# A two-layer graph convolution after a graph attention layer, 6250 nodes and 100000 edges: more buffers for the one-hot matrices and more accumulator banks

## The reference

```python
# GAT: weights a per edge and head (softmax over the edges of one node)
msg = feat_v[src] * a[:, :, None]
rst = jax.ops.segment_sum(msg, dst, num_segments=N)
# GCN layer, twice (x = relu(_gcn_layer(x, W, b, ...)))
h = x @ W
deg = jax.ops.segment_sum(ones, dst, num_segments=n_nodes) + SELF_LOOP_W
dinv = jnp.where(deg > 0, jax.lax.rsqrt(deg), 0.0)
msgs = h[src] * (dinv[src] * dinv[dst])[:, None]
agg = jax.ops.segment_sum(msgs, dst, num_segments=n_nodes)
return agg + h * (SELF_LOOP_W * dinv * dinv)[:, None] + b
```

## Time and profile before

| what | us |
|---|---|
| median of 3 runs | 5063.07 |
| span of the profiled execution | 5032.2 |
| GAT aggregation, about 899 to 2254 | 1355 |
| first GCN aggregation, about 2471 to 3645 | 1174 |
| second GCN aggregation, about 3850 to 5021 | 1171 |

### The profile page before, as it was taken

How to read it: one execution, slowest core, us unless ns; L and a number is a source line. 1 busy time by engine, 2 the same in 40 slices (tenths; PEclk the granted TensorE clock), 3 DMA queues, 4 the chain that set the end, 5 groups by cost and what they waited for, 6 DMA issues and landing times.

```text
span 5032.2 us, 77636 instructions
## 1 busy us (share of the span) xinstructions
PE 3834.1 (76%) x18550; PEld 2250.0 (45%) x18551; DVE 2339.5 (46%) x4398; ACT 2192.4 (44%) x5340; POOL 2436.2 (48%) x2548
## 2 busy tenths in 40 slices
PE   4679998667667667779777777777897777777777
PEld 3369983455555555554323333333343333333333
DVE  5358887556566566668422222222353222222226
ACT  3236542334344444445444444444543444444444
POOL 3510000555555555543466666666503666666666
PEclk8889999888888888889888888899998888888989
DMA  7522325555555555555566665666514666666668
GB/s 247 169 60 59 84 53 182 153 158 156 154 157 152 143 146 146 151 146 196 185 178 181 174 177 170 170 177 174 158 75 144 182 178 179 175 170 172 177 174 305
DMA packets 317266, 803.60 MB, mean 160 GB/s; under 512 B 67665, under 2 KB 97251, under 8 KB 316241
## 3 DMA queue, kind: packets, MB, share of 16 engines
q0 software_dynamic: 193760, 629.95, 43.7%
q1 hardware_dynamic: 94981, 120.30, 7.6%
q10 hardware_dynamic: 28428, 52.40, 3.1%
HBM read 718.21 MB, written 85.04 MB: 160 GB/s over the span
## 4 chain that ended last, share of the span: by engine, by line
PE 56%; another core or an unknown queue 17%; issue 12%; ACT 6%; DVE 3%; ACTq 2%; DMA 2%; DVEq 1%; SPq 1%; POOL 1%; POOLq 0%
PE mm L1661 12%; PE tr L1661 11%; PE mm L1491 7%; PE mm L1638 4%; PE sm L1638 4%; PE mm L1583 4%; PE tr L1583 4%; ACT eler_hots L1392 2%; PE sm L1528 2%; ACT eler_hots L1383 2%; PE tr L1638 2%; PE hist_ps L1638 2%; PE tr L1486 1%; DVE big L857 1%
## 5 line engine op out<-in xcount | busy, mean ns | idle before, releaser
L1250 POOL DMA_INDIRECT edge<-h_tab,src_group x1564 | 1491.3, 954 | 1079.9 <-issue 431.7
L1392 ACT ACTIVATE eler_hots<-eler_hots,ones 128x256 f32<-128x256 f32 x1320 | 663.8, 503 | 1177.8 <-remote 622.4
L1661 PE MATMUL mm<-edge,eler_hots 128*128 x1760 | 923.3, 669 | 308.5 <-ACT eler_hots L1392 152.5
L1661 PE MATMUL tr<-edge,eler_hots 128*128 x1760 | 916.5, 664 | 277.8 <-DVE big L857 109.4
L1250 POOL DMA_INDIRECT rows_wmat<-v_tab,src_group x782 | 739.0, 945 | 636.7 <-DVE edge L831 375.8
L1383 ACT ACTIVATE eler_hots<-iota,ndrel 128x128 f32<-128x128 f32 x2640 | 916.0, 393 | 173.8 <-issue 9.1
L1661 PEld LDWEIGHTS mm<-edge,eler_hots 128*128 128x128 f32 x1760 | 367.4, 214 | 835.9 <-issue 830.7
L1661 PEld LDWEIGHTS tr<-edge,eler_hots 128*128 128x128 f32 x1760 | 364.9, 212 | 799.7 <-issue 799.7
L857 DVE TENSOR_TENSOR big<-big,mm 128x512 f32 x440 | 302.8, 688 | 894.3 <-remote 347.1
L857 DVE TENSOR_TENSOR big<-big,tr 128x512 f32 x440 | 302.7, 688 | 827.8 <-remote 371.0
L1638 PE MATMUL mm<-edge,eler_hots 128*128 128x260 f32 x1176 | 423.3, 446 | 308.7 <-ACT eler_hots L1392 206.5
(11 more groups left out here) (234 smaller groups left out, 3873.8 us busy)
## 6 DMA issues: line engine op xcount, KB each, us to landing
h_tab<-rows_wmat SPq DMA_DIRECT2D x98, 256.0 KB, 2.0
edge<-h_tab,src_group POOLq DMA_INDIRECT x1564
rows_wmat<-low_tab SPq DMA_DIRECT2D x191, 128.0 KB
ht_tab<-rows_wmat SPq DMA_DIRECT2D x49, 256.0 KB
big<-ht_tab ACTq DMA_DIRECT2D x49, 256.0 KB
v_tab<-rows_wmat ACTq DMA_DIRECT2D x49, 256.0 KB
x_tab<-big SPq DMA_DIRECT2D x49, 256.0 KB, 2.1
rows_wmat<-v_tab,src_group POOLq DMA_INDIRECT x782
```

What stands on the lines that cost most here:

```text
L1250: pool.indirect_dma_start(ring[:, 2 * u + c, :], None, tab, bass.IndirectOffsetOnAxis(ap=src_group[:, n:n + 1], axis=0)).then_inc(a["rows_ ...
L1392: act.activation(onehot[:, s.j % 2, :, :], dist[:, :, :], ACT.Relu, bias=ones[:, 0:1], scale=-1.0).then_inc(a["onehot_set"], 1)
L1661: last = pe.matmul(sum_ps[bank][:, :], onehot[:, s.j % 2, n, :], edge[:, ds(slot[0][s.j] + n * D, D)], start=(n == 0), stop=(n == 1))
```

## The change

`hots` is a new tile of 8 KB per partition with eight one-hot buffers; `dist` gets two buffers, in the room that the one-hots leave in `eler_hots`. In the GCN the Relu of step n waits for `step_sum` n - 7 (step n - 8 has been summed) and the Abs of step n for the Relu of step n - 2. The GCN accumulators go round eight banks, so PE waits for `acc_added` of the step eight before. In the GAT the accumulators stay three pairs; there the one-hot is tied to the three `msgs` buffers, whose last 8 columns ACT writes at the same point, and the Relu of step n waits for step n - 3 to be summed. Loops grow where the buffer number has to be fixed in the code: ACT's in the GCN from 4 to 8 steps, PE's in the GAT from 12 to 24.

```diff
+SUMS = 8
+HOTS = 8
...
+        hots = sb("hots", [P, HOTS * 2 * P])
...
-        onehot = eler_hots[:, 0:4 * P].rearrange("p (b c n) -> p b c n", b=2, c=2)
-        dist = eler_hots[:, 4 * P:6 * P].rearrange("p (c n) -> p c n", c=2)
+        onehot = hots[:, :].rearrange("p (b c n) -> p b c n", b=HOTS, c=2)
+        dist = eler_hots[:, 0:4 * P].rearrange("p (b c n) -> p b c n", b=2, c=2)
...
         sum_ps, half_ps = mm + tr, sm + [hist_ps, misc]
+        agg_ps = sum_ps + half_ps
...
-                        w, bank = s.k - LAG, (s.j - LAG) % BANKS
+                        w, bank = s.k - LAG, (s.j - LAG) % SUMS
...
-                        dve.tensor_tensor(big[:, ds(o, D)], big[:, ds(o, D)], sum_ps[bank][:, :], ALU.add).then_inc(a["acc_added"], 1)
+                        dve.tensor_tensor(big[:, ds(o, D)], big[:, ds(o, D)], agg_ps[bank][:, :], ALU.add).then_inc(a["acc_added"], 1)
...
-                    if s.past(1):
-                        act.wait_ge(a["onehot_set"], n)
+                    reuse = MSGS if a["weighted"] else HOTS
+                    if s.past(2):
+                        act.wait_ge(a["onehot_set"], n - 1)
                     for c in range(2):
-                        act.activation(dist[:, c, :], iota[:, :], ACT.Abs,
+                        act.activation(dist[:, s.j % 2, c, :], iota[:, :], ACT.Abs,
...
-                    if s.past(2):
-                        act.wait_ge(a["step_sum"], n - 1)
+                    if s.past(reuse):
+                        act.wait_ge(a["step_sum"], n - reuse + 1)
...
-                    pipelined(act, SP, 4, 0, step, tail=(SP - SETTLED) * bool(settled))
+                    pipelined(act, SP, HOTS, 0, step, tail=(SP - SETTLED) * bool(settled))
...
-                            last = pe.matmul(bank_ps[:, 0:hi - lo], onehot[:, s.j % 2, n, :], msgs[:, s.j % MSGS, n, lo:hi],
+                            last = pe.matmul(bank_ps[:, 0:hi - lo], onehot[:, s.j % HOTS, n, :], msgs[:, s.j % MSGS, n, lo:hi],
...
-                pipelined(pe, SP, 4 * PAIRS, 0, step)
+                pipelined(pe, SP, HOTS * PAIRS, 0, step)
...
-                    if s.past(BANKS):
-                        pe.wait_ge(a["acc_added"], w - BANKS + 1)
+                    if s.past(SUMS):
+                        pe.wait_ge(a["acc_added"], w - SUMS + 1)
                     for n in range(2):
-                        last = pe.matmul(sum_ps[bank][:, :], onehot[:, s.j % 2, n, :], edge[:, ds(slot[0][s.j] + n * D, D)],
+                        last = pe.matmul(agg_ps[bank][:, :], onehot[:, s.j % HOTS, n, :], edge[:, ds(slot[0][s.j] + n * D, D)],
```

More of the change, by code:

```diff
@@ L1390, in step @@
                                        ACT.Copy)
-                    act.activation(onehot[:, s.j % 2, :, :], dist[:, :, :], ACT.Relu,
+                    act.activation(onehot[:, s.j % HOTS, :, :], dist[:, s.j % 2, :, :], ACT.Relu,
                                    bias=ones[:, 0:1], scale=-1.0).then_inc(a["onehot_set"], 1)
@@ L1646, in step @@
                 def step(s):
-                    w, bank = s.k, s.j % BANKS
+                    w, bank = s.k, s.j % SUMS
                     if s.j == 0:
```

## The result

The kernel after takes **5020.13 us** (median of 5 runs, 5009.24 to 5025.08) beside 5060.97 for the kernel before (5 runs, 5045.22 to 5071.13): ratio 0.9923, 95% interval 0.9904 to 0.9943, so 41 us or 0.8% faster. The forecast was 4868, a gain of 195 us. The sign is right, the size is off by a factor of five.

A forecast was written before the change was run, and what follows sets the result against it. POOL's gathers were taken to bound the GCNs, with stalls from late counts of finished sums. Saving 175 us in both GCNs and 20 in the GAT gave 4837 of span, plus 30.9 outside: 4868 us, forecast range 4800 to 4925.

The forecast's parts named there:

- The floor: GCN aggregations: POOL's gathers, 1.251 us each, set the pace at 978 us; 343 us of POOL's standing is excess.
- The loop: GCN stalls: finished sums counted late while gathers flow, so ACT, PE and POOL stop in turn until gathers pause.
- Step (1): GCN: PE makes eight sums without hearing back, so POOL's waits put down to PE go, saving 88.7 us.
- Step (2): GCN: POOL's stops at a full ring fall from 106 to 60 to 78, 2.40 us each, saving 66 to 110.
- a smaller gain: Whole kernel: fewer stops, each longer, giving 4925 to 5053 us; chance 0.07.
- Step (3): GCN: DVE adds up to eight sums at 0.89 us each in time; second distance buffer and longer ACT loop bring nothing.
- GAT, -20 us: GAT: the third one-hot lets PE make one more sum in a late stretch, saving 20 us of at most 73.
- (a): GCN: late stretches end by themselves or don't arise, so all 343 us go, 4700 us; chance 0.17.
- (b): GCN stalls: PE itself stands, so buffers don't help; 5043 to 5063 us, mostly no change; chance 0.13.
- (c): GCN: PE gets half clock more often, up to 194 us more per GCN, 5450 us; chance 0.10.

The follow-up runs named there:

- after_flat: The kernel after with the loops of ACT, PE and DVE in all three aggregations written out; 4884.88 us, 0.9741 of the kernel before.
- paced16: The kernel after with GAT's loops as before and three small POOL memsets behind each GCN gather; 4996.38 us, 0.9963 of the kernel before.
- banks_only: The kernel before with eight GCN accumulator banks and nothing else of the change; 5054.15 us, 0.9992 of the kernel before.
- hots_only: The kernel after with four GCN accumulator banks again, the eight one-hots kept; 0.9930 of the kernel before.
- act_flat: The kernel after with ACT's one-hot loop of both GCNs written out for all 440 steps; 0.9905 of the kernel before.
- bf4: The kernel after with GAT's loops as before and GCN products of the upper two bytes only, made four times; 5026.47 us, 0.9930 of the kernel before.
- narrow: The kernel after with GAT's loops as before and GCN gathers of 512 bytes a row, not 2 KB; 5001.87 us, 0.9881 of the kernel before.
- before_flat: The kernel before with the loops of ACT, PE and DVE in all three aggregations written out; 0.9843 of the kernel before.
- half_gathers: The kernel after with GAT's loops as before and one of each GCN unit's two gathers left out; 4186.98 us, 0.8353 of the kernel before.

## Why the prediction was right and wrong, step by step

**The floor, where it failed.** "POOL should set the pace, at 2.50 x 391 / 440 = 2.22 us a step", so 978 us for a GCN's gathers and 343 us of avoidable standing in both. The 1.251 us were read from 26 gathers after a long pause, and that stretch was itself the beginning of a late one. No kernel with 782 gathers held a mean below 1.441 us over a GCN (after_flat), 1.441 x 781 = 1125 us, and paced16 shows that POOL hardly stands any more once its gathers are paced at 1.444 us. The kernel before, with 1166.7 and 1168.6, was 85 us above this in both GCNs together; the kernel after, with 1147.7 and 1153.1, is 51 above. So, as an estimate from single profiles, the change took 35 of 85 us, where I thought to take 175 of 343. A number that could have warned: the whole stage's mean, 1.494 us a gather, beside a median pitch of 1.251.

**The loop.** Late count, ACT may not write the next one-hot, PE stands, ring full, gathers stop, counts arrive: no run speaks against a link, and banks_only (nothing) with hots_only (about all of the gain) shows that the one-hot was the link that held PE. But I took the late count for a disturbance with a cost of its own. The reading that fits all runs is that it is one of the ways in which too fast gathers are slowed down. Taking a link out changed who stands, and little for how long.

**Step (1), -88.7 us:** wrong in sign. PE-named waits rose by 41 us (169.1 - 128.0) where 88.7 were to go. PE did not make eight sums at 1.72 us: in a late stretch its own register instructions took 700 ns, and after some four sums of it PE went by pairs of matmuls.

**Step (2), 60 to 78 remote waits of 2.4 us:** the number was right at its edge (59), the price was not (3.4 us; 3.1 when the 0.30 us that every gather has anyway is taken off, as in the prediction's 2.4). The prediction named this way to fail, "the late stretch, with POOL freer, just lasts longer at its end", and gave a smaller gain, 4925 to 5053, a chance of 0.07. That case came in. It should have had far more, since nothing in the profile said that a stop has a fixed price.

**Step (3):** not contradicted. DVE's adds come 0.89 us apart in runs, and act_flat, which has no loop of ACT in the GCNs, is not told from the kernel after (0.9905 and 0.9923). No run takes the second distance buffer by itself.

**GAT, -20 us:** most likely wrong in sign, about +16 (5020.13 - 5004.16). POOL's waits for DVE's multiplications grew from 375.8 us to this:

```profile
L1254 POOL DMA_INDIRECT rows_wmat<-v_tab,src_group x782 | 739.0, 945 | 654.2 <-DVE edge L835 405.7 <-issue 213.8 <-DMA v_tab<-rows_wmat 34.8
```

**The rivals.** (a), that the late stretches end by themselves, fell: 59 remote stops were left, where zero would have been its sign. (b), that PE itself stands, was half right: PE's register instructions crawl there, but an uncounted sum really is finished (DVE adds three 0.89 us apart at 2779.24), and with hardly a slow one among them (bf4) the stage was no shorter. The Trainium skill's "SBUF — State Buffer", section "Who interferes with whom", was cited for (b). By narrow its rule on DMA traffic holds here: bytes make no difference. Its sentence that PE and ACT never wait on anyone stands there among rules for the ports of the on-chip memory. Rival (b) read it more widely, and so read it does not hold in these stretches: PE's register instructions took 700 ns while gathers flowed, and 44 when they came at 1.44 us or in half the number. (c), PE at half clock, did not come: the granted clock of the GCNs stayed at 0.88 and 0.90.

## What to carry to other kernels

A pace read from a few instructions in a row is a floor only if something shows that it lasts; set it beside the mean over the stage, and where a stage keeps its length while its waits change places, look for a resource that is paid per item. The quickest test is to slow the suspected leader on purpose: if the stage stays about as long (paced16: 0.19 us more per gather, most of it at no cost), most of the time that was standing before was owed, and no buffer will bring it back. And here writing the loops out, so that the numbers to wait for become constants, was worth more than the buffers: 1.6% alone (before_flat), 2.6% with the change. Why, no run shows.

## What the runs showed of the hardware

- Indirect gathers of this kernel, some 780 in a row, come at 1.44 to 1.51 us each in the mean, whatever their bytes (44 or 176 GB/s) or rows (64 or 128). What stays the same in all these is 16 small packets a gather: narrow's queue had 24896 packets for some 778 gathers, 12448 of them under 512 bytes. Whether these, the gather instruction itself or something else sets the limit is open.
- When gathers come faster than that, the other engines are held up while POOL's own go on every 1.25 us: in the kernel after 217 of 440 finished sums are counted 5 to 15 us late, and register instructions of PE and ACT take about 700 ns, one per 1.4 us on PE, until gathers pause. DVE, SP and POOL show hardly any (10 on DVE in the first GCN of the kernel after). Why is open. Each of these runs carried the recording that the profile is made of, so no run tells whether the recording has a part in it. The number of recorded instructions doesn't set the length: between the first and the last gather of the first GCN there are 10099 in before_flat (1152 us) and 16193 in bf4 (1168 us), and half_gathers has 12317 in 747 us without one sum over 0.7 us late. The Trainium skill, "NOTIFIC — the notification-queue block", section "Overflow: three behaviours, one of which stalls the engine", says that this block holds its producers back rather than lose a record inside; no run here shows that this is the cause.
